# Moving two norms' moments to ScalarE, and three reorderings on TensorE, in a fused attention and spiking feed-forward kernel

## The reference

```python
qkv = layernorm(x) @ W_qkv.T             # q, k, v per head
k = (k - mean(k)) / sqrt(var(k) + eps)   # over the 16 features of a head
# per head a 16 x 16 state, over the 512 tokens:
F = retention * F + coef * outer(v_t, k_t)
y_t = (W_LTM + F) @ q_t
x = x + layernorm(y @ W_o.T)
h = square(relu(layernorm(x) @ W_fc.T))  # 1024 features
d = h @ W_proj.T                         # then 5 spiking steps, counted
x = x + layernorm(spikes(d) / 5)
```

## Time and profile before

| | us |
|---|---|
| median of 3 runs (lowest, highest) | 573.79 (570.6, 579.51) |
| the profiled execution, its time | 574.97 |
| its span, first to last instruction | 573.2 |

### The profile page before, as it was taken

One profiled execution on the slowest core, in us unless ns is written; L12 is line 12 of the kernel. 1 busy time (PEld: TensorE's weight loads), 2 busy tenths in 40 slices (PEclk: granted clock), 3 DMA queues, 4 the chain that ended last, 5 costly groups with the idle time before them and its releaser, 6 DMA issues.

```text
span 573.2 us, 7812 instructions
## 1 busy us (share of the span) xinstructions
PE 474.5 (83%) x2245; PEld 313.6 (55%) x2252; DVE 539.0 (94%) x858; ACT 341.3 (60%) x788; POOL 386.7 (67%) x206
## 2 busy tenths in 40 slices
PE   4683567549989899979998899989997999897992
PEld 2451234225677466736675557756673667565881
DVE  5699999999999999999999999999999999997767
ACT  5461343444565986687767886697758745763331
POOL 1138996587857968696968794897769686783022
PEclk9698687858989899999999998989999999999997
DMA  7475577556573568647685649455942778410002
GB/s 263 138 196 145 145 186 199 138 154 162 136 206 107 144 168 239 179 116 202 175 211 150 172 122 245 122 152 125 288 135 94 183 215 221 134 39 8 29 2 73
DMA packets 54778, 87.64 MB, mean 153 GB/s; under 512 B 5456, under 2 KB 19408, under 8 KB 54736
## 3 DMA queue, kind: packets, MB, share of 16 engines
q1 hardware_dynamic: 54160, 87.12, 56.2%
q10 hardware_dynamic: 576, 0.03, 0.1%
HBM read 78.74 MB, written 8.39 MB: 152 GB/s over the span
## 4 chain that ended last, share of the span: by engine, by line
PE 54%; DVE 18%; issue 12%; POOL 8%; ACT 6%; DMA 1%; SPq 0%; DVEq 0%; POOLq 0%; ACTq 0%
PE p_c L381 13%; PE p_c L411 11%; DVE state L963 9%; PE p_a L311 7%; PE p_y L359 6%; POOL prod L1237 5%; PE p_c L372 4%; PE p_a L332 2%; PE p_y L350 2%; DVE p_u L953 2%; PE p_a L305 2%; POOL x1t L1253 2%; PE p_u L550 1%; DVE yf L1189 1%; PE p_a L341 1%
## 5 line engine op out<-in xcount | busy, mean ns | idle before, releaser
L1237 POOL TENSOR_TENSOR prod<-state,qf 128x1024 f32<-128x1024 f32 x127 | 300.8, 2375 | 120.3 <-DVE state L963 60.2
L963 DVE TENSOR_TENSOR_SCAN state<-ret,p_u 128x512 f32<-128x512 f32 x256 | 308.8, 1207 | 0.0
L953 DVE TENSOR_TENSOR p_u<-vrep,p_k 128x512 f32<-128x512 f32 x256 | 170.9, 673 | 0.1
L381 PE MATMUL p_c<-wproj_sb,ht 128*128 128x256 f32 x448 | 102.0, 381 | 0.0
L381 PEld LDWEIGHTS p_c<-wproj_sb,ht 128*128 128x128 f32 x448 | 83.5, 190 | 16.8 <-issue 5.0
L311 PE MATMUL p_a<-xt,wqkv_s 128*128 128x512 f32 x276 | 85.1, 448 | 5.7 <-POOL xt L1253 2.1
L411 PE MATMUL p_c<-x1t,wfc_s 128*128 128x512 f32 x324 | 82.7, 401 | 2.3 <-ACT hr L684 1.0
L359 PE MATMUL p_y<-prod,summer 128*32 128x512 f32 x512 | 75.5, 664 | 7.9 <-POOL prod L1237 6.5
L311 PEld LDWEIGHTS p_a<-xt,wqkv_s 128*128 128x128 f32 x276 | 55.2, 210 | 46.0 <-issue 18.7
L411 PEld LDWEIGHTS p_c<-x1t,wfc_s 128*128 128x128 f32 x324 | 59.5, 188 | 18.9 <-POOL x1t L1253 3.4
L700 ACT ACTIVATE sign<-yf,drive_sb 128x512 bf16<-128x512 f32 x60 | 38.1, 710 | 0.2
(11 more groups left out here) (188 smaller groups left out, 596.4 us busy)
## 6 DMA issues: line engine op xcount, KB each, us to landing
vrep<-v_rows SPq DMA_DIRECT2D x256, 256.0 KB, 4.4
xa<-in_x SPq DMA_DIRECT2D x9, 512.0 KB, 5.0
v_rows<-vf SPq DMA_DIRECT2D x16, 256.0 KB, 2.9
x<-in_x SPq DMA_DIRECT2D x7, 512.0 KB, 6.9
out<-x SPq DMA_DIRECT2D x7, 512.0 KB, 3.3
ht<-in_w_fc SPq DMA_DIRECT2D x1, 1024.0 KB, 7.3
wproj_sb<-in_w_proj SPq DMA_DIRECT2D x1, 1024.0 KB, 10.2
state<-in_w_qkv SPq DMA_DIRECT2D x1, 512.0 KB, 5.9
```

The source lines that it names most:

```text
L381: last = pe.matmul(p_c[(u + 1) % 2][:, 0:D], ht[:, f, tokens(u)], wproj_sb[:, f, :], start=(f == 0), stop=(f == FT - 1))
L953: v.tensor_tensor(p_u[n % NU][:, :], vrep[:, n % NV, :], p_k[:, :], ALU.mult).then_inc(S["hebb_done"], 1)
L963: v.tensor_tensor_scan(state[:, s % NS, i, :], ret[:, r:r + 1].broadcast_to([P, L]), p_u[n % NU][:, :], 0.0, ALU.mult, ALU.add).then_inc(S ...
L1237: p.tensor_tensor(prod[:, s % NZ, :, :], state[:, s % NS, :, :], qf[:, s // HS, :].unsqueeze(1).broadcast_to([P, 2, L]), ALU.mult).then_in ...
```

## The change

- `statistics` and `moments_of` of norms 2 and 3 are taken out of VectorE's list. ScalarE squares the four tiles with the accumulator instead: `squares_o` in slot 3 (no bias, as the mean is zero), `squares_x1` in slot 7 behind `copy_key` (bias: minus the mean of x). The mean of x is kept for that in three buffers in turn, `minus_mean_x`. `deviation` reads the sums of squares for all norms.
- On ScalarE `deviation(2, b1)` moves from slot 4 to slot 3, `norm1(b)` from slot 3 to slot 4 behind `spread_k`, and `hidden(b2, 7)` from slot 0 to slot 1 behind `square_k(g, 1)`.
- On TensorE `up(b1, 7)` moves from slot 15 to slot 1 of the next iteration, between `project_k(g, 1)` and `key_variance(g, 1)`. `key_scale(g, 1)` moves from slot 5 to slot 4, ahead of `down(b2, 1)`. `key_scale(b, 0)` moves from slot 14, behind `sums(g, 5)`, to slot 13, ahead of them.
- `turn_x1(b1, 1)` writes `p_c0` instead of `p_a`. So it doesn't wait for the copy of `turn_x1(b1, 0)`; it waits for the last `copy_yf` of b2, and `count_spikes(b2, 1)`, which uses the same bank, waits for the copy of it.

```diff
--- before.py
+++ after.py
@@ -111,14 +111,15 @@
         dev = [sb(f"dev{i}", [P, TILES]) for i in range(4)]
         rdev = [sb(f"rdev{i}", [P, TILES]) for i in range(4)]
         nmr = sb("nmr", [P, TILES])
-        squares = {n: sb(f"squares{n}", [P, TILES]) for n in (1, 4)}
+        squares = {n: sb(f"squares{n}", [P, TILES]) for n in (1, 2, 3, 4)}
         spread = {n: sb(f"spread{n}", [P, TILES]) for n in (1, 4)}
         twice_mean = sb("twice_mean", [P, TILES])
         eight = sb("eight", [P, TILES])
         tail_nmr = sb("tail_nmr", [P, TILES])
         passed = sb("passed", [P, TILES, D])
         total = {n: sb(f"total{n}", [P, TILES]) for n in (1, 4)}
-        minus_mean = {n: sb(f"minus_mean{n}", [P, TILES]) for n in (1, 4)}
+        minus_mean = {4: sb("minus_mean4", [P, TILES])}
+        minus_mean_x = [sb(f"minus_mean_x{i}", [P, TILES]) for i in range(3)]
         minus_half = sb("minus_half", [P, TILES])
 
         xa = sb("xa", [P, TILES, D])
@@ -167,8 +168,8 @@
             n1_stats n1_sum n1_mean n1_var n1_dev n1_step n1_done  xt_turned xt_done xt_high xt_low
             k_proj k_sq k_var k_dev k_rdev k_spread k_scale k_done k_bank  v_proj v_done  q_proj q_done
             v_out hebb_done state_done prod_done sum_done y_done
-            o_proj o_done n2_stats n2_var n2_dev n2_step n2_done x1_done
-            n3_stats n3_var n3_dev n3_step n3_done  x1_turned x1t_done x1t_high x1t_low
+            o_proj o_done n2_var n2_dev n2_step n2_done x1_done
+            n3_var n3_dev n3_step n3_done  x1_turned x1t_done x1t_high x1t_low
             up_done relu_done h_done down_done yf_done
             sign_done count_done spk_done n4_stats n4_mean n4_var n4_dev n4_step n4_offset n4_done pool_step res_done
             tail_out tail_x1 tail_var2 tail_dev2 tail_var3 tail_dev3 tail_n3 tail_turned tail_high tail_low tail_up tail_relu tail_h
@@ -315,7 +316,7 @@
             def project_v(b, half):
                 pe.wait_ge(S["xt_low"], at(KT * (b + 1)))
                 pe.wait_ge(S["k_done"], at(2 * b + half))
-                if half == 0: pe.wait_ge(S["x1t_done"], at(KT * (b - 1)))
+                if half == 0: pe.wait_ge(S["x1t_done"], at(KT * (b - 1) - 1))
                 project(b, 2 * D + half * P, "v_proj")
 
             def project_k(b, half):
@@ -385,6 +386,7 @@
             def count_spikes(b, pair):
                 pe.wait_ge(S["sign_done"], at(2 * b + pair + 1))
                 pe.wait_ge(S["yf_done"], at(TILES * b + 3 + pair))
+                if pair == 1: pe.wait_ge(S["x1t_done"], KT * (b + 2))
                 for j in range(STEPS):
                     last = pe.matmul(p_c[(pair + 1) % 2][:, :], ident_b[:, :], sign[:, pair, j, :, :],
                                      start=(j == 0), stop=(j == STEPS - 1))
@@ -394,9 +396,11 @@
                 pe.wait_ge(S["n3_done"], at(TILES * (b + 1)))
                 pe.wait_ge(S["k_done"], min(2 * (b + 2), 2 * B))
                 pe.wait_ge(S["xt_done"], min(KT * (b + 3), KT * B))
-                pe.wait_ge(S["x1t_done"], at(KT * b + t))
+                pe.wait_ge(S["x1t_done"], at(KT * (b - 1) + t + 1))
+                if t == 1: pe.wait_ge(S["yf_done"], at(TILES * b))
+                bank = p_a if t == 0 else p_c[0]
                 for u in range(TILES):
-                    last = pe.transpose(p_a[:, tokens(u)], oo[:, u, t * P:(t + 1) * P], ident_sb[:, :])
+                    last = pe.transpose(bank[:, tokens(u)], oo[:, u, t * P:(t + 1) * P], ident_sb[:, :])
                 last.then_inc(S["x1_turned"], 1)
 
             def up(b, f):
@@ -481,26 +485,27 @@
                     if now:
                         if s == 0: project_v(g, 1)
                         if s == 1: project_k(g, 1)
+                        if s == 1 and two_before: up(b2, 7)
                         if s == 2: key_variance(g, 1)
                     if before and s == 2:
                         project_out(b1, 0)
                         project_out(b1, 1)
                     if now and s == 3: project_q(g, 1)
-                    if now and s == 5: key_scale(g, 1)
                     if after and s == 6: turn_x(b, 0)
+                    if now and s == 4: key_scale(g, 1)
                     if two_before and 3 <= s < 7: down(b2, s - 3, before)
                     if after:
                         if s == 7: turn_x(b, 1)
                         if s == 10: project_v(b, 0)
                         if s == 11: project_k(b, 0)
                         if s == 13: project_q(b, 0)
-                        if s == 14: key_scale(b, 0)
                     if two_before and s == 8: count_spikes(b2, 0)
                     if two_before and after and s == 10: count_spikes(b2, 1)
                     if before and s == 9:
                         turn_x1(b1, 0)
                         turn_x1(b1, 1)
                     if after and not before and s == 11: key_variance(b, 0)
+                    if after and not before and s == 13: key_scale(b, 0)
                     if before and after:
                         if s == 10: up(b1, 0)
                         if s == 11:
@@ -510,10 +515,9 @@
                         if s == 13:
                             up(b1, 3)
                             up(b1, 4)
+                            key_scale(b, 0)
                         if s == 14: up(b1, 5)
-                        if s == 15:
-                            up(b1, 6)
-                            up(b1, 7)
+                        if s == 15: up(b1, 6)
                     if not after:
                         if s == 10: up_first_pair(b1)
                         if 11 <= s < 14:
@@ -586,13 +590,9 @@
 
             def deviation(n, b):
                 act.wait_ge(S[f"n{n}_var"], at(b + 1))
-                if n in (1, 4):
-                    eps = eps_sb[:, 0:1] if n == 1 else eps_sb[:, 2:3] if b == LAST - 1 else eps_sb[:, 1:2]
-                    nc.scalar.activation(dev[n - 1][:, :], squares[n][:, :], ACT.Sqrt, bias=eps, scale=1.0 / D).then_inc(
-                        S[f"n{n}_dev"], 1)
-                else:
-                    nc.scalar.activation(dev[n - 1][:, :], moments[n - 1][:, :, 1], ACT.Sqrt, bias=eps_sb[:, 0:1]).then_inc(
-                        S[f"n{n}_dev"], 1)
+                eps = eps_sb[:, 0:1] if n < 4 else eps_sb[:, 2:3] if b == LAST - 1 else eps_sb[:, 1:2]
+                nc.scalar.activation(dev[n - 1][:, :], squares[n][:, :], ACT.Sqrt, bias=eps, scale=1.0 / D).then_inc(
+                    S[f"n{n}_dev"], 1)
 
             def total_x(b):
                 act.wait_ge(S["x_in"], 16 * (b + 1))
@@ -600,13 +600,13 @@
                     last = nc.scalar.activation(passed[:, u, :], xa[:, u, :], ACT.Identity, accum_out=total[1][:, u:u + 1])
                 last.then_inc(S["n1_sum"], 1)
                 act.wait_ge(S["n1_sum"], b)
-                nc.scalar.activation(minus_mean[1][:, :], total[1][:, :], ACT.Identity, scale=-1.0 / D).then_inc(
+                nc.scalar.activation(minus_mean_x[b % 3][:, :], total[1][:, :], ACT.Identity, scale=-1.0 / D).then_inc(
                     S["n1_mean"], 1)
 
             def squares_x(b):
-                act.wait_ge(S["n1_mean"], b)
+                act.wait_ge(S["n1_mean"], b + 1)
                 for u in range(TILES):
-                    last = nc.scalar.activation(passed[:, u, :], xa[:, u, :], ACT.Square, bias=minus_mean[1][:, u:u + 1],
+                    last = nc.scalar.activation(passed[:, u, :], xa[:, u, :], ACT.Square, bias=minus_mean_x[b % 3][:, u:u + 1],
                                                 accum_out=squares[1][:, u:u + 1])
                 last.then_inc(S["n1_var"], 1)
 
@@ -673,9 +673,24 @@
                 copy(p_c[(t + 1) % 2][:, :], oo[:, 2 * t:2 * t + 2, :].rearrange("p u d -> p (u d)"), "o_proj",
                      2 * b + t + 1, "o_done")
 
+            def squares_o(b):
+                act.wait_ge(S["o_done"], 2 * (b + 1))
+                for u in range(TILES):
+                    last = nc.scalar.activation(passed[:, u, :], oo[:, u, :], ACT.Square,
+                                                accum_out=squares[2][:, u:u + 1])
+                last.then_inc(S["n2_var"], 1)
+
+            def squares_x1(b):
+                act.wait_ge(S["n1_mean"], b + 1)
+                act.wait_ge(S["x1_done"], b + 1)
+                for u in range(TILES):
+                    last = nc.scalar.activation(passed[:, u, :], x1[b % 2][:, u, :], ACT.Square,
+                                                bias=minus_mean_x[b % 3][:, u:u + 1], accum_out=squares[3][:, u:u + 1])
+                last.then_inc(S["n3_var"], 1)
+
             def copy_x1t(b, t):
                 act.wait_ge(S["x1t_low"], at(KT * (b - 1) + t + 1))
-                copy(p_a[:, :], x1f[:, t, :], "x1_turned", KT * b + t + 1, "x1t_done")
+                copy((p_a if t == 0 else p_c[0])[:, :], x1f[:, t, :], "x1_turned", KT * b + t + 1, "x1t_done")
```

(25 more changed lines are left out.)

## The result

The change makes the kernel slower: 580.86 us median against 574.22, 20 runs each, ratio 1.008 with a 95% interval of 1.0057 to 1.0104, so clear of noise and under 2%. The forecast was 571.0 us, in a range from 562 to 578; the sign was wrong, and the time lies outside the range. The profiled execution took 584.27 us (span 582.4), near the top of the runs (574.28 to 585.16), so the account of the loss further down goes by a second profile of the same kernel, f1, with 578.72 us.

A forecast was written before the change was run, and what follows sets the result against it. Path V sets the 61.0 us iteration, path T has about 2 us of slack; -1.9 in g=1, -1.5 into g=2, +0.7 in g=3 to 6, -0.1 in g=7 make -2.8 us: median 571.0 us, range 562 to 578.

The forecast's parts named there:

- Rival 1: VectorE sets the time and its removed work is simply gone: 23.7 us less, 550 us; chance 0.07.
- Product 15: GpSimd's product that `sums(b1, 7)` on TensorE waits for until 279.85: some 2.0 us of TensorE idling there.
- Key scale ahead: TensorE, `key_scale(b, 0)` before `sums(g, 5)`: key normalization 0.99 us earlier, sums 0.41 us later, path T up to 0.41 longer.
- Two banks: TensorE's x1 transposes: the second's 0.86 us wait goes, but is covered by GpSimd's second low_x1; worth 0.
- `up` 7 fills the hole ahead of the variance: TensorE: 1.4 us of work fills the 1.38 us wait for the squares; the hole moves ahead of `sums(b1, 7)`.
- TensorE without a gap to `down(2)`: TensorE after the key variance, 0.24 us late there: no further wait up to `down(2)`.
- Rival 3: TensorE's clock: slow stretches in all five iterations instead of two, +4.5 us, 575.5 us; chance 0.14.
- path V: VectorE's slots, ScalarE's third deviation, GpSimd's 12.1 us, `up(b1, 0)`, key scale, back to VectorE; sets the 61.0 us.
- Rival 2: path T is shorter, the 2.0 us ahead of `sums(b1, 7)` not idle: 563 to 567 us likely; chance 0.16.
- path T: `up` 0 to 4, sums, GpSimd's products, TensorE to the third `down`, ScalarE's copies; about 2 us of slack before.
- The copy of xt(0) ... still stands behind it: ScalarE: the copy that GpSimd's 12.1 us hang on stays behind the third deviation, so moving the third norm's statistics gains nothing.
- which from now on has no slack: Said of path T: `squares_x1` puts 2.1 us of work where ScalarE had 2.07 us of idling.

The follow-up runs named there:

- f1: The changed kernel itself, unaltered, run again on another chip: 579.07 us, 1.0085 of before.
- f4: Kernel before with only the moments of both norms moved to ScalarE, and batch 1's key scale in slot 13: 572.17 us, 0.997 of before.
- e1: Changed kernel with copy_y(b1, 1) ahead of hidden(b2, 7) on ScalarE: 567.94 us, 0.990 of before.
- h3: g1 with the copy of y ahead of the hidden tile, as in e1: 572.2 us, 0.998 of before.
- f2: e1 plus, on GpSimd, product 15 ahead of the feed-forward addition, which moves to slot 0 of the next iteration: 561.57 us, 0.977 of before.
- e4: Changed kernel with the third norm's moments back on VectorE, no squares_x1: 0.998 of before for the faster group of runs; median of all twelve 586.48 us.
- g3: g2 with copy_xt(b, 0) ahead of squares_x1 and the third deviation on ScalarE: 568.82 us, 0.986 of before.
- g1: Changed kernel with both moments back on VectorE, keeping TensorE's order, hidden tile 7 and two banks as changed: 589.62 us, 1.023 of before.
- h1: g1 with eight identity transposes into p_c1 ahead of TensorE's wait for y: 575.16 us, 1.0025 of before.
- g4: e1 with both x1 transposes through p_a as before: 569.27 us, 0.988 of before.
- h2: h1 with twenty more identity transposes into p_c0 ahead of the wait for the signs: 576.09 us, 1.004 of before.
- g2: f2 with the output store moved to slot 5 and the reload of x to slot 7 of SyncE's list: 561.0 us, 0.972 of before.
- f3: Changed kernel with eight identity transposes into p_c1 ahead of TensorE's wait for y: 577.11 us, 1.005 of before.

## Why the prediction was wrong, point by point

**Right.** VectorE's freed 3.4 us lie beside the path: busy 88%, waits of 2.17 and 2.98 us for the first and third deviation (about 2 each were forecast), and moving the moments off VectorE gives 0.4 us per iteration (f4) or 0.64 (e1 against h3). Rival 1, with the Trainium skill's rule beside it ("Perfetto Trace Analysis", "Identifying the Most-Contended Engine"), would have had 550 us. This case disagrees with the rule: the engine at 94% worked 24 us less, and the time went up by 0.8%; the moments alone (f4) take off 0.3%.

Product 15: 1.78 us of TensorE waiting against 2.0 forecast; f2 shows that it is on the path. Key scale ahead: 0.45 us per iteration against 0.41. Two banks: 0. `up` 7 fills the hole ahead of the variance, and the hole moves: so it did.

**The step that failed** is "TensorE without a gap to `down(2)`", in the sum. The prediction said that hidden tile 7 "now stands behind the key squares and ahead of `copy_y` and the key deviation", followed the deviation to VectorE, and did not follow the copy to `project_out(b1, 0)`, which waits for it. With before's times: tile 7 can't start on ScalarE until `up` 7 is through at 283.75, takes 1.17, the copy 0.57, so the projection can't start until 285.6 or so instead of 284.7. It was all in the rows. The term, put at nothing, is a wait of 1.05 us, and 1.21 us per iteration when it is taken out (e1). It turns four iterations of +0.17 into five of +1.04.

How this adds up is seen from the starts of the output projections, in us after (+) or ahead of (-) those of the kernel before, up to the end of the span:

```
                      g=2    g=3    g=4    g=5    g=6    g=7    end
changed, in f1       -3.2   -1.7   -0.6   +0.3   +1.9   +2.9   +3.7
changed, as shown    -2.8   -2.9   +1.4   +3.9   +3.9   +8.2   +9.2
```

The forecast had -3.4 in g=2 and -2.8 at the end. In f1 the start is nearly as forecast, with luck in it: 1.7 us of its 3.2 are an instruction that no edit touches (last section). The five distances to g=7 are +6.2 us instead of +0.7, and 5 x 1.04 = 5.2 of them are the undisturbed iteration. The rest is +0.8 instead of -0.1, as one more projection, the last batch's in g=7, fell under the low clock:

```profile
523.65 5.41 PE L536 MATMUL p_u<-wo_sb,yt 128*128 128x256 f32 x16 [0.75 <-ACT yt L628]
```

**The clock** is the smaller part in f1: the same two iterations as before have the low stretches, at 1.7 us instead of 1.3 each. It is what sets the profiled execution of the result apart: 5.5 us above f1, with slow projections in g=3, 4, 6 and 7, and in g=4 and 7 project_k (2.80 and 2.74 us instead of 1.65) and `up` 7 (2.01 and 2.07 instead of 1.54) slow as well. Rival 3 had the mechanism and about its price (1.5 us against 1.7), but behind the wait for product 15 and with 0.14; it came mostly behind the wait for y, which rival 3 didn't know, and in f1 in no more iterations than before. Its 575.5 us counted no such wait. "Before, path V covers part of it" holds in that a slow stretch need not cost what it adds: in g=5 of before the projection takes 5.20 us instead of 3.70, and some 25 us behind it sums and project_v are slow as well (1.90 and 2.41 instead of 1.06 and 1.66), but the wait for the signs that follows falls from 1.8 to 0.3 us, and the iteration is 1.3 longer.

**Too pessimistic**, hidden by the above: without the copy of y the iteration is 60.83, not 61.2. With a queue untangled on GpSimd as well it is 59.5 and less. Rival 2 (path T shorter by up to 2 us) named the right place and about the price (1.3 to 1.4 us in f2), but the change as made doesn't have it: its sign of being right, a wait below 1 us there, is absent.

**"The copy of xt(0) ... still stands behind it", "which from now on has no slack":** half right. Taking `squares_x1` out (e4) gave 0.5 us of the 2 that it takes, and moving it behind the copy (g3) cost 1.5. The wait for the signs stood 0.24 us behind.

**Open.** Why the low clock comes in one execution at a place and not in the next. Shown is: g1, with the wait of 1.05 us for y, has it in each iteration of g=3 to 6; h3, without that wait, has none; h1, with 0.9 us of work in it, has a single one. The wait alone isn't enough: in f1 it stands in iterations with and without the low clock, and e4's profile has g1's two waits, 1.05 and 2.63 us, in every iteration of g=3 to 6 and no low stretch there. g1 ran on another chip than h1 and h3, and was not run on theirs; the ratios are each against before on its own chip, but that the pattern of g1 has nothing to do with its chip is not shown.

## What to carry to other kernels

When a step moves within an in-order queue, list every instruction that now stands behind it, and for each of them who waits; the one that you don't look at is the price. Freeing an engine at 94% of 3.4 us per iteration gave 0.4 to 0.6 us, as other engines with about 2 us of slack stood beside it, and the gain lay in two swaps of neighbours (a copy ahead of a tile, a product ahead of an addition). A wait on TensorE can cost more than its length, as the clock may go down with it: in this kernel a new wait of 1 us was 1 us and, in some iterations, 1.7 to 3 more.

## What was not expected of the hardware

One VectorE instruction of 128 x 2 elements, the scaling of the column sums once per execution, takes 0.17 us in the changed kernel and 1.91 us in the one before; it took 1.89 in g4, 2.73 in h2 and 2.75 in g2, and 0.17 in all other runs. The kernel before:

```profile
L931 DVE TENSOR_SCALAR osum<-osum x1: 1910/1910/1910, 79.8 to 79.8; 128x2 f32<-128x2 f32 x1
```

The first iteration is 59.3 us with the short one and 61.0 to 61.9 with the long one. No edit touches this instruction, its cause is open, and it is 1.7 us in favour of the changed kernel in the pairs of profiles compared here.

That 0.9 us of useless transposes in a wait makes the order-only kernel 2% faster (h1 against g1, both against before on their own chip) was the largest surprise; the granted clock of the two windows, 1.00 and 0.80, shows by what. In the changed kernel, which had fewer low stretches to lose, the same transposes gave 0.4% on one chip (f3 against f1), within what the intervals leave open.
